# Second attention: one score tile in every fifteenth unit goes from PSUM by VectorE to GpSimd's power operation

## The reference, cut to what matters

```python
H, D = (16, 8)
q = (x @ wq + bq).reshape(B, Sq, H, D).transpose(0, 2, 1, 3)
k = (y @ wk + bk).reshape(B, -1, H, D).transpose(0, 2, 1, 3)
v = (y @ wv + bv).reshape(B, -1, H, D).transpose(0, 2, 1, 3)
scores = jnp.einsum('bhqd,bhkd->bhqk', q, k) / jnp.sqrt(jnp.asarray(D, x.dtype))
attn = jax.nn.softmax(scores, axis=-1)
out = jnp.einsum('bhqk,bhkd->bhqd', attn, v)
```

## Time and profile before

| | us |
|---|---|
| median of 3 runs (1854.46 to 1858.78) | 1857.36 |
| the profiled execution | 1853.31 |
| its span, first to last instruction | 1851.5 |
| the stage of the change, about 932 to 1667 | 735 |

### The profile page before, as it was taken

How to read it: one execution, slowest core, us unless ns; L and a number is a source line. 1 busy time by engine, 2 the same in 40 slices (tenths; PEclk the granted TensorE clock), 3 DMA queues, 4 the chain that set the end, 5 groups by cost and what they waited for, 6 DMA issues and landing times. The chain is left out here.

```text
span 1851.5 us, 22757 instructions
## 1 busy us (share of the span) xinstructions
PE 1582.9 (85%) x8261; PEld 603.4 (33%) x8261; DVE 854.8 (46%) x2331; ACT 1373.1 (74%) x1441; POOL 169.9 (9%) x154
## 2 busy tenths in 40 slices
PE   6789788898998993776789999999999999985996
PEld 4463354554554552533211111111111111113442
DVE  7768999999999997473400000000000000003223
ACT  5737687888887874313289999999999999982332
POOL 4840211111111101000000000000000000000000
PEclk8869899999999996787689999999999999997998
DMA  3430968979769679350000004000500000003000
GB/s 103 144 117 0 184 150 177 202 155 210 174 151 230 152 179 241 78 152 7 18 1 1 1 1 63 13 1 1 75 1 1 1 1 1 1 1 98 0 1 12
DMA packets 69263, 143.41 MB, mean 77 GB/s; under 512 B 21993, under 2 KB 40642, under 8 KB 68218
## 3 DMA queue, kind: packets, MB, share of 16 engines
q0 software_dynamic: 13616, 75.73, 20.5%
q1 hardware_dynamic: 55098, 65.30, 13.2%
q10 hardware_dynamic: 432, 0.85, 0.1%
HBM read 52.65 MB, written 13.99 MB: 36 GB/s over the span
## 5 line engine op out<-in xcount | busy, mean ns | idle before, releaser
L1936 ACT ACTIVATE ex<-ps 128x1536 f32<-128x1536 f32 x536 | 721.9, 1494 | 6.0 <-PE ps L1890 6.0
L1905 PE MATMUL ps<-ex,V 128*9 128x512 f32 x3200 | 419.8, 597 | 0.5 <-ACT ex L1936 0.4
L850 PE MATMUL ps<-K,qst 128*128 128x512 f32 (+1 forms) x832 | 392.9, 604 | 30.7 <-ACT srow L920 20.7
L1890 PE MATMUL ps<-Q,K 52*128 52x512 bf16 (+1 forms) x1632 | 322.8, 385 | 39.1 <-ACT ex L1936 34.2
L1946 DVE COPY o<-ps 9x512 f32<-9x512 f32 x32 | 22.0, 687 | 714.2 <-PE ps L1909 713.5
L1051 DVE MAX8 cand<-srow 128x8 f32<-128x200 f32 (+1 forms) x1024 | 318.7, 359 | 8.7 <-ACT srow L920 8.6
L1011 DVE SCALAR_TENSOR_TENSOR both<-srow,top,both 128x1536 f32<-128x1536 f32 (+1 forms) x128 | 239.4, 1870 | 21.2 <-ACT both L937 21.0
L920 ACT COPY srow<-ps 128x1024 f32<-128x1024 f32 (+1 forms) x224 | 205.1, 924 | 46.1 <-PE ps L850 45.7
L937 ACT ACTIVATE both<-srow,shift 128x1536 f32<-128x1536 f32 (+1 forms) x128 | 209.4, 1638 | 23.2 <-DMA both<-both 21.8
L1890 PEld LDWEIGHTS ps<-Q,K 52*128 52x128 bf16 (+1 forms) x1632 | 60.7, 94 | 448.1 <-ACT ex L1936 433.1
L850 PEld LDWEIGHTS ps<-K,qst 128*128 128x128 f32 x832 | 150.8, 198 | 166.5 <-issue 116.1
(11 more groups left out here) (333 smaller groups left out, 1087.2 us busy)
## 6 DMA issues: line engine op xcount, KB each, us to landing
both<-both POOLq DMA_DIRECT2D x69, 768.0 KB, 8.9
v_ring<-v_rows SPq DMA_DIRECT2D x84, 256.0 KB, 6.3
both<-both POOLq DMA_DIRECT2D x23, 898.0 KB, 13.1
K<-k_parts SPq DMA_DIRECT2D x48, 204.0 KB
k_parts<-kl SPq DMA_DIRECT2D x12, 384.0 KB, 2.6
V<-v_rows SPq DMA_DIRECT2D x4, 900.0 KB, 6.7
v_rows<-v1g SPq DMA_DIRECT2D x12, 288.0 KB, 3.8
srow<-v_rows SPq DMA_DIRECT2D x1, 3200.0 KB, 17.5
```

The costliest lines, as they stand in the source:

```text
L850: last = M.matmul(ps[:, BANK_OF[item] + b, 0:c1 - c0], qst[:, h, :], K0[:, c0:c1], start=True, stop=True)
L1890: last = M.matmul(out, K1[rows_, quad % 2, hh // 2, keys], Q1[rows_, 4 * quad + hh, tb * TB:(tb + 1) * TB], start=True, stop=True, tile_po ...
L1905: last = M.matmul(out, V1[:, quad % 2, g, VW * j:VW * j + VW], ex1[:, slot(w, 4 * g + j), :], start=g == 0, stop=False, tile_position=(0, ...
L1936: C.activation(ex1[:, s:s + NBANK, :], ps[:, b:b + NBANK, :], ACT.Exp)\
```

## The change

In units 6, 21, 36 and 51 of each pass (`OWN`) ScalarE makes the exponential of two tiles only, 128x1024. The third tile (20, 65, 110 or 155) is copied from PSUM to `score` by VectorE, with a floor at -118, and GpSimd raises 2 to it, into one of eight slots of `power`. For that the scores carry a factor log2(e), and ScalarE's exponential multiplies by ln 2. The value groups leave out the matmul of such a tile; the four of a pass are summed together by `own_values`, after the scores of unit 66 (`LATE_AT`). VectorE reads the sums of pass w - 1 at the start of pass w, ahead of the copies of that pass. The scores of a unit wait for the copy too, where one is on the bank.

```diff
-EXP_RANGE = 60.0
+LOG2E = float(np.log2(np.e))
+LN2 = float(np.log(2.0))
+EXP_RANGE = 60.0 * LOG2E
...
-        SC1 = float(DH1) ** -0.5
+        SC1 = float(DH1) ** -0.5 * LOG2E
...
+        BATCH = 4
+        power = sb(b8, "power", [P, 2 * BATCH, TB])
+        score = sb(b8, "score", [P, 2, TB])
+        two = sb(b8, "two", [P, 1])
...
+        EVERY, FIRST_U, BATCHES = 15, 6, 1
+        OWN = [FIRST_U + EVERY * i for i in range(BATCH * BATCHES)]
+        LATE_AT = {OWN[BATCH * (b + 1) - 1] + (EVERY if b == BATCHES - 1 else EVERY + 1): b for b in range(BATCHES)}
+        OWN_TILE = {NBANK * u + NBANK - 1: i for i, u in enumerate(OWN)}
...
+        LOW2 = -118.0
+
+        def own_before(k):
+
+            w, u = divmod(k, NU)
+            return w * len(OWN) + sum(1 for o in OWN if o < u)
...
+                PL.memset(two[:, :], 2.0).then_inc(S("two_ready"), 1)
+                pool.wait_ge(S("two_ready"), 1)
+                for m in range(NPASS * len(OWN)):
+                    done = m // BATCH
+                    pool.wait_ge(S("own_read"), m + 1)
+                    if done >= 2:
+                        pool.wait_ge(S("power_used"), done - 1)
+                    PL.tensor_tensor(power[:, m % (2 * BATCH), :], two[:, 0:1].to_broadcast([P, TB]), score[:, m % 2, :], ALU.pow)\
+                        .then_inc(S("powered"), 1)
...
                     if w * NU + u >= 2:
                         pe.wait_ge(S("exped1"), w * NU + u - 1)
+                        if own_before(w * NU + u - 1):
+                            pe.wait_ge(S("own_read"), own_before(w * NU + u - 1))
...
                     for j in range(4):
+                        if 4 * g + j in OWN_TILE:
+                            continue
...
+                def own_values(w, b):
+
+                    quad = w // NB
+                    pe.wait_ge(S("powered"), w * len(OWN) + BATCH * (b + 1))
+                    for i in range(BATCH * b, BATCH * (b + 1)):
+                        n = NBANK * OWN[i] + NBANK - 1
+                        g, j = divmod(n, 4)
+                        last = M.matmul(ps[32 * j:32 * j + VW, 6 + w % 2, :], V1[:, quad % 2, g, VW * j:VW * j + VW],
+                                        power[:, (w * len(OWN) + i) % (2 * BATCH), :], start=False, stop=False,
+                                        tile_position=(0, 32 * j))
+                    last.then_inc(S("power_used"), 1)
...
+                        if u in LATE_AT:
+                            own_values(w, LATE_AT[u])
...
-                        C.activation(ex1[:, s:s + NBANK, :], ps[:, b:b + NBANK, :], ACT.Exp)\
-                            .then_inc(S("exped1"), 1)
+                        n = NBANK - 1 if u in OWN else NBANK
+                        C.activation(ex1[:, s:s + n, :], ps[:, b:b + n, :], ACT.Exp, scale=LN2).then_inc(S("exped1"), 1)
...
+                def own_scores(w, i):
+
+                    m = w * len(OWN) + i
+                    dve.wait_ge(S("scored1"), w * NU + OWN[i] + 1)
+                    if m >= 2:
+                        dve.wait_ge(S("powered"), m - 1)
+                    V.tensor_scalar(score[:, m % 2, :], ps[:, bank(w, NBANK * OWN[i] + NBANK - 1), :], LOW2, None, ALU.max)\
+                        .then_inc(S("own_read"), 1)
```

More of the change, by code:

```diff
@@ L1839, in program @@
         assert NTILE % NBANK == 0 and NSLOT % NBANK == 0
+        EVERY, FIRST_U, BATCHES = 15, 6, 1
+        OWN = [FIRST_U + EVERY * i for i in range(BATCH * BATCHES)]
+        LATE_AT = {OWN[BATCH * (b + 1) - 1] + (EVERY if b == BATCHES - 1 else EVERY + 1): b for b in range(BATCHES)}
+        OWN_TILE = {NBANK * u + NBANK - 1: i for i, u in enumerate(OWN)}
+        assert max(LATE_AT) < NU and len(LATE_AT) == BATCHES and NBANK * FIRST_U >= 4
+        LOW2 = -118.0
+        def own_before(k):
+            w, u = divmod(k, NU)
+            return w * len(OWN) + sum(1 for o in OWN if o < u)
         def last_tile(g):
@@ L1935, in _, with read_sums @@
                         s, b = slot(w, NBANK * u), bank(w, NBANK * u)
-                        C.activation(ex1[:, s:s + NBANK, :], ps[:, b:b + NBANK, :], ACT.Exp)\
-                            .then_inc(S("exped1"), 1)
+                        n = NBANK - 1 if u in OWN else NBANK
+                        C.activation(ex1[:, s:s + n, :], ps[:, b:b + n, :], ACT.Exp, scale=LN2).then_inc(S("exped1"), 1)
             @block.vector
             def _(dve):
-                dve.wait_ge(S("o1_zero"), 1)
-                for w in range(NPASS):
+                def read_sums(w):
                     quad, tb = divmod(w, NB)
@@ L1947, in _ @@
                                       ps[32 * j:32 * j + VW, 6 + w % 2, :]).then_inc(S("o1_read"), 1)
+                def own_scores(w, i):
[5 more added lines that the diff above has]
+                        .then_inc(S("own_read"), 1)
+                dve.wait_ge(S("o1_zero"), 1)
+                for w in range(NPASS):
+                    if w:
+                        read_sums(w - 1)
+                    for i in range(len(OWN)):
+                        own_scores(w, i)
+                read_sums(NPASS - 1)
     q1s.close()
```

## The result

The changed kernel takes 3858.09 us (median of 4 runs, 3855.74 to 3865.38) against 1855.91 for the kernel before on the same chip: **2.081 times as long, 95% interval 2.078 to 2.085**, 2002 us more. The forecast was 1861.8 and the range ended at 1873.

The account below looks back on a forecast made before the run. ScalarE was taken as the bound, but five units by way of TensorE (6.675 us) lay only 0.04 us under ScalarE's 6.7125. Terms -1.3 + 5.4 + 0.3 = +4.4 us on 1857.36 gave 1861.8 us, range 1853 to 1873.

Parts of the forecast that it names:

- GpSimd's power: On GpSimd between own tiles: about 20.1 us free, 19 for a pass's last; no wait taken, so no cost.
- Rival B: At unit 66: power lasts over 20 us, TensorE waits; 1882 us at 20.5, 1930 at 22; chance 0.12.
- the 4.4 of the rest: Whole kernel, power costing nothing: own tiles -1.3, late group +5.4 at boundaries and +0.3 at the end, sum +4.4 us.
- the late group: After unit 66's scores: four own tiles' sum delays the next scores 0.77 us at seven boundaries, +5.4, and +0.3 at stage end.
- own tiles: In windows of five units: TensorE's order decides, so each of 32 shorter exponentials gives only 0.04 us, -1.3 us.
- the group with three matmuls in place of four: TensorE's value groups without the own tile: leaving one column group out shortens no wave, 0.
- VectorE's copy: Own tile out of PSUM: 0.75 us, ending before the shortened exponential of about 1.02 does, so 0.
- rival C: Each unit's scores: the second wait costs TensorE time; at 0.02 us each +5.4 more, 1867.2 us; chance 0.08.
- rival A: Window of five: ScalarE keeps what it is spared, 13.7 us; in full -8.0, 1849.4 us; chance 0.13.
- Rival D: Pass boundary: the late group costs half, as TensorE's 0.84 us there holds idle time; +1, 1858.4 us; chance 0.07.
- A sign that was named wrongly: ScalarE over the run: busy time down by 13 us and idle time up by more.
- The sign beside it: After own units' exponentials of about 1.02 us: ScalarE waits hand back 0.39 of the 0.43 us within four units.

Follow-up runs that it names:

- e2: The changed kernel with a product in place of GpSimd's power: stage 736.7 us against 732.9 before, kernel 1.0007 times the kernel before.
- e3: The changed kernel with a product for the power and the late sum of own tiles left out: stage 730.6 us, 0.9990 times the kernel before.
- e1: The kernel before with the two constants alone (scores times log2(e), exponential scaled by ln 2): stage 732.9 us, 0.9993 times the kernel before.
- e5: The changed kernel with the power over 128 of 512 columns, the rest summed as ones: stage 775.7 us, kernel 1897.4 us in one run.
- e4: The changed kernel with the power over 64 of 512 columns, the rest ones: stage 736.1 us, 1.0014 times the kernel before.
- e6: The changed kernel with four kinds of power over 64 columns (plain, 8 partitions, zero exponents, full tile of twos): stage 736.7 us, kernel 1858.8 us in one run.
- e9: Against the kernel before: 14 own tiles a pass, exponential on VectorE with a GpSimd step, value groups two units later, 18 slots, no late group: 1832.76 us, ratio 0.9877.

## Why the prediction was wrong, point by point

**The step that failed** is that on GpSimd's power: "From below the price is one of these and costs nothing; from above, eight of the dearest in a row, 19.8 us, reach the wait. I take no wait". The power takes 81.9 us, 33 of the dearest row and 79 products of its own shape (e2). The eight were no bound: nothing in the rows ties a power to additions, and the number was drawn where the wait began. With the price open from above and its effect growing by 32 us for each further microsecond, the range had to reach far up or say that it could not be closed, and 0.12 for the rival was too little. By the runs a column of the power takes 0.159 us. The 12 cycles for an element of branching code that the Trainium skill gives (GPSIMD Engine Reference, section 3.1), from which the prediction's estimate of 5.1 us came, are no guide to this operation: at the 1.2 GHz of that page's section 1 the 0.159 us are 191 cycles.

**Rival B** is what came about, beyond its examples. Its formula, 4 x (p - 20.1) + 0.9 a pass, gives 8 x 248.2 = 1985 us at p = 81.92, 1990 with the 4.4 of the rest; the stage grew by 2003. The mechanism, the place and the growth per microsecond were right, and so was the room, to within a microsecond: 20.1 and 19 us were taken, 19.94 and 19.84 are in the trace of e2. What the formula left out is the slower TensorE after each standstill: from the late group to the next pass's first power 13.1 us pass here (1273.16 to 1286.23), where e2 has 11.55 from the late group to its first product (1024.72 to 1036.27), 1.5 us more a pass and up to 2.1 at later ones. The waits by way of the two buffers of `score` add nothing to this sum, since GpSimd works on through them; they only move where TensorE stands still.

**What the rest of the change costs** was right: +4.4 worked out, +3.8 measured without the power (e2). By parts, without the 0.5 us of the earlier clock in e3: the late group 5.7 worked out, 5.6 measured (e2 against e3); own tiles -1.3 against -1.8; scale 0 and 0.0 (e1); the group with three matmuls in place of four no shorter, 0.98 us to the next scores in both. So the overhead for each matmul of the Trainium skill's page TensorEngine Tiling (Array Packing), section "Instruction Overhead", which would have given 1.6 to 3.2 us, does not show. VectorE's copy 0.75 taken, 0.69 measured, nobody waits for it in e2. The second wait on TensorE (rival C) costs nothing that these runs show, and rival A's 13.7 us are not to be had with one tile in fifteen units (e3: 1.8). Rival D is out as well: the boundary is 0.78 us longer, not half of that, and by its own terms (half of 5.7, less 1.3) its sum would have been +1.5 and not +1.

**A sign that was named wrongly:** ScalarE's busy time was to fall by 13 us. It fell by 2.1 in the change and by 5.4 in e2 (1367.7). Busy time is that of at least one instruction; successive exponentials overlap, and where the next one is late that overlap is gone. The stage's length and the steps between the ends show the gain, the busy time does not. The sign beside it held: of the 0.43 us that an own unit ends earlier, 0.38 is handed back within four units (e2).

**What stays open** is what a power does in its 0.159 us a column, and why the product's 1.04 us is so far under the 2.47 of the earlier trace rows.

## What to carry to other kernels

An operation that no row of the trace shows has no upper bound from rows of other operations. If the plan rests on it, measure it alone, over few columns, before anything is built around it: 64 and 128 columns, 10.5 and 20.7 us, give the price of a column and with it that of 512.

A wait costs more than its length where the engine that waited comes back at a lower clock: in e5 24.1 us of waiting made the stage 39.6 us longer.

What sparing the busiest engine brings is read from the loop through its neighbour, not from its busy share: here five units by way of TensorE were 0.04 us shorter than by way of ScalarE. Spare it once in every such loop (0.2 us a tile) or leave it; spared now and then it gives 0.05 and the added work costs more.

## What the runs showed of the hardware that was not expected

- GpSimd's power takes 0.33 us and 0.159 us for each column, 81.9 us for 512, the same over 8 partitions and 128, for zeros and for scores, with a repeated column and a full tile (e4 to e6). Its product takes 1.04 us for 512 columns (e2).
- After a standstill of 3.5 us TensorE's granted clock is 0.50, 1.2 GHz, in the stretches that follow (e5, 1028 to 1034), and a value group takes 1.90 us for 1.04.
- One kind of VectorE operation was slower beside GpSimd. In e9 two VectorE operations of one input and constants on a 128x512 tile take 427 ns (L1973, in all 112 cases ahead of GpSimd's step) and 716 (L1976, in all 112 beside it). L1976 has a second constant, but that alone hardly slows it: in the kernel before, L453 does 4096 columns with two in 2341 ns, 0.57 ns a column for 1.40. That GpSimd is the cause is argued from this, not shown: no run has L1976 without GpSimd's step beside it. Operations of two inputs take 0.69 us beside the step (L1975) and after it (L1983). GpSimd's step takes 2.43 us, always with VectorE beside it; what it takes alone was not measured. The timeline of one tile:

```profile
1304.34 0.43 DVE L1973 TENSOR_SCALAR turn<-score 128x512 f32<-128x512 f32 x1
...
1304.85 2.43 POOL L1882 TENSOR_SCALAR scale<-turn 128x512 int32<-128x512 f32 x1 [2.82 <-DVE turn L1973]
...
1305.53 0.72 DVE L1976 TENSOR_SCALAR poly<-part 128x512 f32<-128x512 f32 x1
```

  The Trainium skill, GPSIMD Engine Reference, section 1, names SBUF interfaces shared with VectorE, with contention where VectorE works in a mode with two ports or has two inputs in SBUF. The 427 and 716 ns agree with the first; of the second the 0.69 us beside and after the step show nothing.
